# A merged attention and FP4 feed-forward kernel: late tiles back to the old order, scales ahead of the tails, one small operation moved to ScalarE, and a rounding mask walked in halves

## The reference, cut to what matters

```
k = elu(x @ Wk + bk) + 1;  k = k / sqrt(sum(k * k) + 1e-6)      # per head of 16
q = elu(x @ Wq + bq) + 1;  v = x @ Wv + bv
attn = q @ (k^T v), per head;  y = x + attn @ Wo + bo
x = layernorm(x + layernorm(y) * gamma + beta)

scale = max(max|x| over 16 / 6, 1e-12);  x = fp4_grid(x / scale) * scale   # weights alike
h = silu(x @ w_gate^T) * (x @ w_up^T)                            # 704 wide
h = quantised like x, block by block;  x = layernorm(x + h @ w_down^T)
```

## Time and profile before

| | us |
|---|---|
| timed runs | 700.04, 700.3, 703.6 |
| profiled execution; its span | 697.06; 695.3 |
| busy over the span: PE, DVE, ACT, POOL | 667.59, 569.91, 531.97, 614.78 |
| first phase and merged pairs, 0 to 207.41 | PE busy 202.82 |
| steps 0 to 10, 207.41 to 286.88 (79.47) | PE busy 75.54 |
| steps 11 to 33, 286.88 to 453.15 (166.27) | PE busy 165.51 |
| steps 34 to 54, 453.15 to 604.66 (151.51 to the start of step 55) | PE busy 151.51 |
| steps 55 to 62, 604.66 to 660.23 (55.57) | PE busy 52.38 |
| from step 63 on, 660.23 to 695.33 (35.10) | PE busy 19.84 |

### The profile page before, as it was taken

One profiled execution on the slowest core, in us unless ns is written; L12 is line 12 of the kernel. 1 busy time (PEld: TensorE's weight loads), 2 busy tenths in 40 slices (PEclk: granted clock), 3 DMA queues, 4 the chain that ended last, 5 costly groups with the idle time before them and its releaser, 6 DMA issues.

```text
span 695.3 us, 14463 instructions
## 1 busy us (share of the span) xinstructions
PE 667.6 (96%) x4178; PEld 583.7 (84%) x4178; DVE 569.9 (82%) x1437; ACT 532.0 (77%) x1060; POOL 614.8 (88%) x919
## 2 busy tenths in 40 slices
PE   8999999999999899999999999999999999999964
PEld 6888888888877799889898998999989899987863
DVE  6678778776879888898898998989899898988752
ACT  5677777766677667788888888888888888888761
POOL 3988898988889999889999999999999999998663
PEclk9999999999999999999999999999999999999996
DMA  8543443344301111465655666557765576533640
GB/s 276 182 137 137 137 141 118 129 156 161 107 32 33 60 38 41 94 111 120 171 125 111 109 144 162 126 111 116 147 139 94 97 121 115 105 65 68 97 101 30
DMA packets 58726, 79.32 MB, mean 114 GB/s; under 512 B 32854, under 2 KB 37912, under 8 KB 58648
## 3 DMA queue, kind: packets, MB, share of 16 engines
q1 hardware_dynamic: 58228, 78.27, 47.3%
q10 hardware_dynamic: 420, 0.13, 0.1%
HBM read 44.90 MB, written 26.08 MB: 102 GB/s over the span
## 4 chain that ended last, share of the span: by engine, by line
PE 58%; POOL 19%; issue 10%; DVE 4%; DMA 4%; ACT 2%; SPq 1%; POOLq 0%; DVEq 0%; ACTq 0%
PE banks L469 15%; PE banks L470 14%; PE banks L471 14%; POOL arena L1264 5%; PE banks L586 4%; POOL arena L1297 3%; POOL arena L1286 3%; DMA resid<-scales_scratch 3%; PE banks L616 3%; POOL lnbuf L1273 3%; PE banks L507 2%; POOL arena L1267 2%; PE banks L480 2%; DVE actT_lo L1076 1%; PE banks L493 1%
## 5 line engine op out<-in xcount | busy, mean ns | idle before, releaser
L469 PE MATMUL banks<-wgu_hi,actT_lo 128*128 128x512 f32 (+1 forms) x384 | 145.6, 379 | 1.6 <-DVE resid L936 1.1
L470 PE MATMUL banks<-wgu_lo,actT_hi 128*128 128x512 f32 (+1 forms) x384 | 143.6, 374 | 0.0
L471 PE MATMUL banks<-wgu_hi,actT_hi 128*128 128x512 f32 (+1 forms) x384 | 143.3, 373 | 0.0
L469 PE MATMUL banks<-wd_hi,actT_lo 128*128 128x256 f32 x320 | 102.0, 319 | 4.0 <-DVE actT_lo L1076 4.0
L471 PE MATMUL banks<-wd_hi,actT_hi 128*128 128x256 f32 x320 | 91.7, 287 | 0.0
L470 PE MATMUL banks<-wd_lo,actT_hi 128*128 128x256 f32 x320 | 91.5, 286 | 0.0
L1264 POOL TENSOR_TENSOR arena<-arena 128x704 f32<-128x704 f32 x64 | 90.2, 1410 | 0.6 <-DVE arena L1054 0.6
L469 PEld LDWEIGHTS banks<-wgu_hi,actT_lo 128*128 128x128 f32 x384 | 72.3, 188 | 14.0 <-DVE actT_lo L1069 1.6
L471 PEld LDWEIGHTS banks<-wgu_hi,actT_hi 128*128 128x128 f32 x384 | 72.1, 188 | 10.6
L470 PEld LDWEIGHTS banks<-wgu_lo,actT_hi 128*128 128x128 f32 x384 | 72.4, 188 | 9.9
L1286 POOL TENSOR_TENSOR arena<-wo_sb,resid 128x1024 f32<-128x1024 f16 (+1 forms) x28 | 59.9, 2138 | 21.1 <-DMA wo_sb<-arena 20.9
(11 more groups left out here) (138 smaller groups left out, 2010.7 us busy)
## 6 DMA issues: line engine op xcount, KB each, us to landing
xs<-x_plus_scratch SPq DMA_DIRECT2D x32, 512.0 KB, 4.3
resid<-scales_scratch SPq DMA_DIRECT2D x28, 512.0 KB
x_plus_scratch<-xs SPq DMA_DIRECT2D x24, 512.0 KB, 2.9
arena<-in_L_attn_x_dram SPq DMA_DIRECT2D x32, 256.0 KB, 3.6
out_dram<-arena SPq DMA_DIRECT2D x32, 256.0 KB, 6.3
x_plus_scratch<-arena SPq DMA_DIRECT2D x4, 512.0 KB, 2.9
x_plus_scratch<-resid SPq DMA_DIRECT2D x4, 512.0 KB, 4.6
resid<-in_L_attn_x_dram SPq DMA_DIRECT2D x4, 256.0 KB, 6.0
```

The source lines that it names most:

```text
L469: nc.tensor.matmul(dst, sl, mh, start=(k == 0), stop=False, skip_group_check=shared)
L470: nc.tensor.matmul(dst, sh, ml, start=False, stop=False, skip_group_check=shared)
L471: last = nc.tensor.matmul(dst, sh, mh, start=False, stop=(ended and k == n - 1), skip_group_check=shared)
```

## The change

Seven things change. (1) `by_dma` ends at n = 56: 22 tiles go by DMA where 28 did. (2) From t = 57 on the order is that of the steps before 6 again (`late(t)` false): turn ahead of the tails, `high_x` ahead of silu 1, `low_x` ahead of gated 1; besides, `high_h` and `low_h` of n from 58 on are called with the x parts, at the end of the step before, and from t = 56 on POOL dequantises n = t + 2 at the end of its step. (3) In the steps whose n = t + 3 goes by DMA, PE does `scales_turn` and `attend` ahead of the tails, and ACT copies the scales ahead of silu 1. (4) The negated means move from POOL to ACT: a new `root_means(t + 1)` behind silu 1, which waits for the aggregates of step t; it is called from t = -8 on, so in the merged pairs too. (5) The last chunk of scales is written by one broadcast transfer instead of two. (6) The mask of `cut` has views with the 32-wide halves of each line outermost. (7) The waits are counted accordingly.

```diff
-        BY_DMA = 12
+        BY_DMA, DMA_END = 12, 56
         def by_dma(n):
-            return joint(n) and n >= BY_DMA and (n - BY_DMA) % 2 == 0
+            return BY_DMA <= n < DMA_END and (n - BY_DMA) % 2 == 0
-        SHIFT = 6
+        SHIFT, UNSHIFT = 6, 56
+        def late(t):
+            return SHIFT <= t <= UNSHIFT
+        def h_with_x(n):
+            return n > UNSHIFT + 1
...
@@ SP, repeat_scales
-                for k in range(2):
-                    sp.dma_start(s_turned[k * half:(k + 1) * half, VC - 1, :],
-                                 sT[whole:whole + half, :]).then_inc(sT_out, 16)
-                sp.wait_ge(sT_out, 3 * 16 * (i + 1))
+                sp.dma_start(s_turned[:, VC - 1, :].rearrange("(k g) t -> g k t", k=2),
+                             sT[whole:VB, :].unsqueeze(1).broadcast_to([half, 2, P])).then_inc(sT_out, 16)
+                sp.wait_ge(sT_out, 2 * 16 * (i + 1))
@@ PE, step
-                if joint(t + 1) and t < SHIFT:
-                    turn(t + 1)
-                if there(t):
-                    gate_up(t, 2)
-                if joint(t + 1) and t >= SHIFT and not by_dma(t + 1):
+                if joint(t + 1) and not late(t):
                     turn(t + 1)
                 if by_dma(t + 3):
                     scales_turn(t + 3)
-                if there(t + 9):
+                    attend(t + 9)
+                if there(t):
+                    gate_up(t, 2)
+                if joint(t + 1) and late(t) and not by_dma(t + 1):
+                    turn(t + 1)
+                if there(t + 9) and not by_dma(t + 3):
                     attend(t + 9)
@@ ACT
+            def root_means(t):
+                act.wait_ge(agg_s, aggregated(t - 1))
+                after(act, root_s, rooted(t - 1))
+                nc.scalar.activation(nm[:, :], mv[:, t % 2, :, 0], ACT.Copy, scale=-1.0).then_inc(nm_s, 1)
             def step(t):
-                if there(t - LAG):
+                if there(t - LAG) and not h_with_x(t):
                     high_h(t)
...
-                if there(t + 1) and t < SHIFT:
+                if by_dma(t + 3):
+                    scales_copy(t + 3)
+                if there(t + 1) and not late(t):
                     high_x(t + 1)
+                if there(t + 1 - LAG) and h_with_x(t + 1):
+                    high_h(t + 1)
                 if there(t):
                     silu(t, 1)
-                if there(t + 1) and t >= SHIFT:
+                if FIRST + 2 <= t + 1 <= LAST + 1:
+                    root_means(t + 1)
+                if there(t + 1) and late(t):
                     high_x(t + 1)
-                if by_dma(t + 3):
-                    scales_copy(t + 3)
@@ DVE, cut
-                nc.vector.tensor_scalar(lines(vqc[n % 2].bitcast(U16)[:, a:b]), vqb[n % 2][:, a // RW:b // RW, 0:RW],
+                nc.vector.tensor_scalar(vqc[n % 2].bitcast(U16)[:, a:b].rearrange("p (r h c) -> p h r c", h=2, c=RW // 2),
+                                        vqb[n % 2][:, a // RW:b // RW, 0:RW].rearrange("p r (h c) -> p h r c", h=2),
                                         ROUND_MASK, None, ALU.bitwise_and).then_inc(round_s, 1)
@@ POOL, roots
-                nc.gpsimd.tensor_tensor(nm[:, :], mv[:, s, :, 0], mone[:, :].broadcast_to([P, 3]), ALU.mult).then_inc(nm_s, 1)
@@ POOL, step
-                elif joint(t + 1) and t > SHIFT:
+                elif late(t) and t > SHIFT:
                     dequantise(t + 1)
...
-                if joint(t + 2) and t < SHIFT:
+                if joint(t + 2) and not SHIFT <= t < UNSHIFT:
                     dequantise(t + 2)
```

More of the change, by code:

```diff
@@ L284, in by_dma @@
         def by_dma(n):
-            return joint(n) and n >= BY_DMA and (n - BY_DMA) % 2 == 0
+            return BY_DMA <= n < DMA_END and (n - BY_DMA) % 2 == 0
         def earlier_by_dma(n):
-            return max(0, (min(n, T + LAG) - BY_DMA + 1) // 2)
+            return max(0, (min(n, DMA_END) - BY_DMA + 1) // 2)
         def turned_on_pe(n):
@@ L786, in scales_copy @@
                 act.wait_ge(sT_ps, i + 1)
-                after(act, sT_out, 3 * 16 * i)
+                after(act, sT_out, 2 * 16 * i)
                 nc.scalar.activation(sT[:, :], ps[0:VB, scales_bank(n), 0:P], ACT.Copy).then_inc(sT_s, 1)
@@ L1139, in step @@
                     aggregate(1, t, have + n3 + n1 + 1)
-                if there(t + 1) and 0 <= t < SHIFT:
+                if there(t + 1) and t >= 0 and not late(t):
                     low_x(t + 1)
+                if there(t + 1 - LAG) and h_with_x(t + 1):
+                    low_h(t + 1)
                 if there(t):
```

## The result

The changed kernel takes 726.07 us (median of 6 runs, 725.23 to 728.21), the kernel before 703.48 in the same comparison (6 runs, 700.04 to 708.13): the ratio is 1.0332, 95% interval 1.029 to 1.0375. It was to be 704.4, with a range of 697 to 712, so the prediction is wrong, and on the slower side. The third rival, given 0.1, came to 721.8.

The account below looks back on a forecast made before the run. PE's own work was taken to bound steps 34 to 54, with up to 18 us to gain in the last steps. 4.4 + 4.6 - 1.2 + 3.6 + 1.2 - 8.5 = +4.1 gave 701.2 profiled, 704.4 median, range 697 to 712.

Parts of the forecast that it names:

- The third rival: Steady part: L1286 settles right ahead of the odd step's mask in every pair, 1.0 a pair; total 721.8, chance 0.1.
- The mask in halves: +3.6 us in the steady part: Odd steps: the narrow mask becomes the fast kind and POOL's L1286 sometimes holds it; 0.17 a pair, 21 pairs.
- so the gain there is nothing: Steady part: scales sent early spare POOL's dequantising its wait, but PE waited for none of it; no gain.
- +0.21 us a pair: Steady pairs: scales and attention ahead of the tails delay the low part of h, then PE's turn; 22 pairs, +4.6.
- -1.2: Steps 12 and 22, already long, lose their cause with the shorter way of the scales: 0.55 + 0.61 us.
- +4.4: Negated means on ACT wait for DVE's aggregates: +1.9 us in pairs 28 to 31, +2.5 at the hand-over to step 0.
- +1.2: Steps 4 to 9: two or three masks in halves held by POOL about a microsecond each, half of it covered.
- The second rival: Halves do not change the kind of mask, so no blocking; 4.8 less than the sum, total 699.6, chance 0.2.
- -8.5: Last steps: old order from step 57, no DMA tiles from 56; +0.7 in steps 55 to 62, the rest afterwards.
- -9.2: From step 63 on: DMA waits and slow-clock stretches go, 8.4 us, and 0.8 for ACT's copy of turned h.
- 700.3: Median of the timed runs before, 3.2 above the profiled 697.06; used to turn 701.2 into the forecast median.
- the first rival: Faster: gain of the last steps stands, waits ahead absorbed as DVE's aggregates come early; 692.6, chance 0.2.

Follow-up runs that it names:

- e12: The changed kernel with one wait more: POOL's dequantising starts behind the wide mask in steps that have one; 709.25 us, ratio 1.011.
- e1: The changed kernel with the old views of the mask instead of the halves, all else as changed; 722.93 us, ratio 1.027.
- e2: The changed kernel with scales and attention behind the tails again on PE and the scales' copy behind high x on ACT; 700.84 us, ratio 0.996.
- e7: e5 with the scales' transpose alone ahead of the tails and the scales' copy ahead of silu 1; 701.87 us, ratio 0.999.
- e9: e5 with one wait more on POOL: its dequantising starts behind the wide mask in steps that have one; 686.56 us, ratio 0.978.
- e10: e7 with one wait more on POOL: its dequantising starts behind the wide mask; 686.56 us, ratio 0.978.
- e11: The kernel before with one wait more on POOL: its dequantising starts behind the wide mask, nothing else; 697.83 us, ratio 0.994.
- e4: The changed kernel with one wait more: POOL's scaling of h starts behind the wide mask in steps that have one; 714.83 us, ratio 1.016.
- e8: The kernel before with the negated means on ACT, nothing else; 708.53 us, ratio 1.011.
- e3: The changed kernel with the negated means back on POOL; 722.99 us, ratio 1.026.
- e5: The kernel before with only the new order of the last steps, no DMA tiles from 56 on, and one broadcast of the last scales; 690.11 us, ratio 0.984.
- e6: The kernel before with the mask walked in halves, nothing else; 711.18 us, ratio 1.012.

## Why the prediction was wrong, step by step

**The steady part, the step that failed.** "The mask in halves: +3.6 us in the steady part" was worked out for the odd step's narrow mask, as a result of the halves, at 0.17 a pair, "near the lower end". Measured are 20.3 us (changed against e12), or 0.9 a pair. The mechanism behind it was named, that L1286 "no longer waits for its transfers" and so POOL comes earlier, and so was the fact that a mask of the fast kind waits for POOL. But three things in it were wrong. The mask that is held is the wide one of the even step, which was of the fast kind already; the operations that hold it are the scaling and the dequantising behind L1286, moved up with it; and the halves have hardly a part in it (345.0 in e1 against 347.0). The third rival had the right price, 1.0 a pair, for the wrong place. And of the early scales I wrote "so the gain there is nothing": they were not neutral but the cause (e2, e7). What I should have followed is POOL's whole order once its transfers land earlier, one position after the other, against every mask of the fast kind. The earlier trace rows had a wide mask of 1.44 in step 10 on its second pair.

**The late tails: right for the even step, nothing for the odd one.** "+0.21 us a pair" were 0.38 in most pairs of e12, half of it where I had put it: its even steps take 7.77 and more instead of 7.58. The tails come 0.98 late (silu 1 at 4.99 instead of 4.01), since beside the 0.79 the first product behind the attention loses some 0.2; and the odd step pays as well, 0.2 (7.00 instead of 6.81), by the low part of x, which I had not followed.

**"-1.2" for steps 12 and 22** did not come. In the kernel before, the wide mask of step 12 took 1.47, held like those above; only step 22 came from late transfers. In the changed kernel both are long (8.64 and 8.19), the one cause having taken the other's place; with the wait, in e9 and e10, both take 7.58. In e11, which has the wait but not the one broadcast of the last scales, step 22 still takes 8.04.

**The merged pairs and the hand-over: the wait right, the sum near by luck.** +4.4 forecast, 5.3 measured (changed, e2, e4 and e8), none without the means on ACT (e3); in e1 and e12 it was 6.7 and 6.8, since step 0 took 10.05 and 10.14 there, at a clock of 0.66. The split was off: up to the last `k_exps` 5.0 instead of 1.9, of which 1.6 fell in pairs 24 to 27, where I had put nothing, and the hand-over 0.3 instead of 2.5. Step 0 starts 1.3 sooner behind the last `k_exps` than before and lasts 1.6 longer, at a clock of 0.80, for which I had no term. The two errors all but cancel.

**Steps 1 to 10: right in kind, without the clock.** +1.2 forecast, 3.3 measured. Some 1.7 are held masks: without the halves, but with a stretch at 1.2 GHz in step 4 as well, e1 has 73.9 and e5 74.0 against 75.7. The other 1.6 are that stretch, which all six kernels with halves show, and of the eight without them e1 and e5 alone. A mask of 960 behind POOL's scaling in step 5 of the profile after:

```profile
249.70 1.40 POOL L1284 TENSOR_TENSOR arena<-arena 128x704 f32<-128x704 f32 x1 [0.37 <-DVE arena L1071]
250.40 0.97 DVE L1080 TENSOR_SCALAR arena<-arena 128x960 uint16<-128x960 uint16 x1
```

In the earlier trace rows the same pair of operations overlapped, for all of the mask's 0.64 and not for 0.55. That the halves make the narrow mask one of the fast kind was right: 0.64 before and 0.644 in e1 beside POOL's work, 0.97 here. The second rival took its condition from a rule that I applied wrongly. By the Trainium skill, VectorE: DVE Perf Modes, section Mode 2×_2P, an odd outermost dimension passes too where source and destination have the same. The trace of before has the narrow mask's source as 15 lines of 64 but its destination as one run of 960, so they are not the same, and the rule leaves this mask out of the fast kind, as measured; with halves outermost both have 2.

**The last steps: right by two errors.** -8.5 forecast, -8.7 measured. The order alone gives -11.0 (e5): -9.3 from step 63 on, against the -9.2 that I wrote, and -1.7 in steps 55 to 62, where I wrote +0.7. The halves give back 2.4 (e1), which I had not counted. That these two cancel was luck.

**The base.** 700.3 was the median of three runs; over the later runs before stands at 702 to 704.5, and e11 points to steps in POOL's early state as one reason.

**A misread column.** The 137.74 us that I gave DVE in the earlier trace rows is the busy time of PE's weight loads; DVE has 136.28 and idles 15.2 us, not 14. Only the case for the first rival used it, and no term of the sum.

## What to carry to other kernels

Before a transfer is made to land earlier, ask what its landing late kept apart: here it held POOL's long operations behind a mask on DVE, and the 8.4 us that POOL waited for it up to step 54, on an engine that does not bound the kernel, was protection. When two engines can hold each other for a whole operation, their order should be set by a semaphore (one `wait_ge` took the changed kernel's ratio from 1.033 to 1.016 in e4 and to 1.011 in e12) and not left to arrival times. A view of the trace that groups one operation by shape, with its mean against its shortest, shows in one line whether it is held.

## What the runs showed that I had not expected

The steady loop has two states with the same code, an early POOL at 8.1 to 8.7 us per even step and a late one at 7.58, and an execution can move from one to the other in its course (e5 at step 25). Five of the profiled executions leave the early state, and in each the masks of the steady part come free right behind one long wait of POOL for these transfers: 1.79 us in step 13 (before), 2.36 in step 13 (e2), 1.94 in step 15 (e8), 2.26 in step 23 (e6), 2.01 in step 25 (e5). In the changed kernel, e1, e3 and e7, whose longest such wait is 1.15, they never do. What keeps POOL early is argued only: POOL is busy 145.06 of 151.51 us in the earlier trace rows, 13.8 of each pair's 14.39, and a pair with a held mask, 15.1 to 15.7 long, gives it more time to run ahead. An operation of POOL that follows a held mask is longer too: the scaling behind the mask of e5's step 18 took 1.58 us instead of 1.39. And the start of an execution, up to the first `k_exps`, varied by 2.9 us over profiles with the same code there.
